# Weight columns of the v projection in a windowed-attention block: 128 token columns per pair of windows in place of 114

## What is computed

```
xn  = layernorm(x)                                  # over the 192 channels
xw  = windows of 7x7 of roll(xn, -3, -3)            # 1024 windows of 49 tokens
q, k, v = xw @ qkv_w + qkv_b                        # 6 heads of 32
o   = softmax(q k^T * scale) v                      # within a window
x   = x + roll back(o @ proj_w + proj_b)
x   = x + gelu(layernorm(x) @ mlp_w1 + mlp_b1) @ mlp_w2 + mlp_b2
```

## Time and profile before

| | |
|---|---|
| median of 3 runs | 2993.93 us (2991.17 to 2994.59) |
| profiled execution | 2994.5 us, span from first to last instruction 2992.4 us |
| TensorE matmuls busy | 2942.3 us, 98% |
| TensorE weight loads busy | 2873.1 us, 96% |
| VectorE busy | 2669.3 us, 89% |
| ScalarE busy | 2276.4 us, 76% |
| GpSimd busy | 1434.7 us, 48% |
| mean granted clock of TensorE | 0.992 |

### The profile page before, as it was taken

The page is one execution under the profiler, slowest core; times in us unless marked ns, Lnnn a source line. Parts: engine busy times, 40 slices in busy tenths (PEclk is TensorE's granted clock), DMA queues, the critical chain, the costliest instruction groups (busy, mean ns, idle before and its releaser), DMA issues.

```text
span 2992.4 us, 115822 instructions
## 1 busy us (share of the span) xinstructions
PE 2942.3 (98%) x43446; PEld 2873.1 (96%) x43446; DVE 2669.3 (89%) x6802; ACT 2276.4 (76%) x4493; POOL 1434.7 (48%) x1678
## 2 busy tenths in 40 slices
PE   6999999999999999999999999999999999999997
PEld 5999999999999999999999999999999999999997
DVE  5899999999999999999999999999999999999994
ACT  3777777777777777777777777777777777877775
POOL 2445454554544455454444545445444554544452
PEclk8999999999999999999999999999999999999998
DMA  1010011001001000100100010010011001001000
GB/s 48 21 31 26 24 28 29 24 25 31 25 24 30 27 24 26 30 24 24 30 26 24 27 29 24 24 31 25 24 28 28 24 26 30 25 24 30 27 21 17
DMA packets 109325, 79.78 MB, mean 27 GB/s; under 512 B 7294, under 2 KB 108782, under 8 KB 109294
## 3 DMA queue, kind: packets, MB, share of 16 engines
q1 hardware_dynamic: 107682, 77.18, 9.6%
q10 hardware_dynamic: 1612, 2.16, 0.2%
HBM read 40.78 MB, written 38.54 MB: 27 GB/s over the span
## 4 chain that ended last, share of the span: by engine, by line
PE 98%; ACT 1%; DVE 1%; ACTq 1%; issue 0%; DVEq 0%
PE ps L855 35%; PE ps L858 16%; PE ps L962 5%; PE ps L886 5%; PE ps L927 5%; PE ps L928 5%; PE ps L935 5%; PE ps L982 5%; PE ps L936 5%; PE ps L929 5%; PE ps L818 3%; PE ps L826 2%; PE ps L943 2%; PE ps L947 1%; PE ps L828 1%
## 5 line engine op out<-in xcount | busy, mean ns | idle before, releaser
L394 POOL TENSOR_TENSOR gl<-g,gh 128x392 fp32r<-128x392 f32 x512 | 566.9, 1129 | 308.5 <-ACT gh L704 308.5
L855 PE MATMUL ps<-zh,w 128*128 128x392 f32 x3072 | 698.7, 342 | 0.6 <-ACT zh L666 0.6
L855 PEld LDWEIGHTS ps<-zh,w 128*128 128x128 f32 x3072 | 551.4, 188 | 0.8 <-ACT zh L666 0.8
L279 POOL TENSOR_TENSOR prob<-prob,rcp 128x588 f32<-128x588 f32 x128 | 152.0, 1187 | 750.2 <-DVE rcp L593 750.2
L698 ACT ACTIVATE g<-ps,biasf 128x392 f32<-128x392 f32 x768 | 396.9, 592 | 131.0 <-PE ps L855 131.0
L855 PE MATMUL ps<-zh1c,wqkv 128*128 128x392 f32 x1536 | 362.6, 345 | 4.0 <-DVE zh1c L452 4.0
L704 ACT ACTIVATE gh<-g 128x392 fp32r<-128x392 f32 x768 | 355.5, 551 | 0.0
L386 POOL CAST zh<-zh1c 128x392 fp32r<-128x392 f32 x256 | 133.7, 522 | 444.9 <-DVE z L442 428.9
L584 DVE TENSOR_TENSOR gl<-g,gh 128x392 fp32r<-128x392 f32 x256 | 289.2, 1168 | 18.3 <-ACT gh L704 18.3
L858 PE MATMUL ps<-wqkv,zh 128*114 128x192 f32 x2048 | 288.4, 268 | 2.5 <-DVE prob L550 2.0
L855 PEld LDWEIGHTS ps<-zh1c,wqkv 128*128 128x128 f32 x1536 | 281.4, 190 | 5.7 <-issue 4.3
(11 more groups left out here) (111 smaller groups left out, 7556.9 us busy)
## 6 DMA issues: line engine op xcount, KB each, us to landing
xin<-in_x SPq DMA_DIRECT2D x128, 147.0 KB
out<-yo SPq DMA_DIRECT2D x128, 147.0 KB
xin<-in_x SPq DMA_DIRECT2D x128, 71.2 KB
out<-yo SPq DMA_DIRECT2D x128, 71.2 KB
xin<-in_x SPq DMA_DIRECT2D x128, 54.8 KB
out<-yo SPq DMA_DIRECT2D x128, 54.8 KB
xin<-in_x SPq DMA_DIRECT2D x128, 18.8 KB
out<-yo SPq DMA_DIRECT2D x128, 18.8 KB
```

The lines of the kernel that those rows point to most:

```text
L394: pool.tensor_tensor(gl[:, m, :], g[:, m, :], gh[:, m, :].bitcast(F32), ALU.subtract)\
L855: last = pe.matmul(dst, cols(w, part), act_, start=(n == 0), stop=(n == 4))
```

## The change

v's stationary operand takes the whole two fields of 64 token columns, 128, where it took 114 (113 and one more); the output is all 128 partitions of the bank, where it was 114. Nothing else is different; what reads v (`values`, line 692) still reads 114 rows.

```
             for p in range(PAIRS):
                 if p % 2 == 0:
                     wait(pe, s_sub, 3, i, p // 2 + 1)
-                last = project(ps[0:PAIR + 1, V + p // 2, 256 * (p % 2):256 * (p % 2) + C], zh1, zl1, wqkv,
+                last = project(ps[:, V + p // 2, 256 * (p % 2):256 * (p % 2) + C], zh1, zl1, wqkv,
                                lambda w, part: w[:, part, 2 * C:3 * C],
-                               tokens=slice(2 * WIDE * p, 2 * WIDE * p + PAIR + 1))
+                               tokens=slice(2 * WIDE * p, 2 * WIDE * (p + 1)))
             last.then_inc(v_done, 1)
```

## The result

The changed kernel takes 3014.33 us (median of 5 runs, 3014.0 to 3016.66) against 2993.93 before, 20.4 us slower; the ratio on record is 1.0072, 95% interval 1.0061 to 1.0084 (the two medians alone give 1.0068). One further run of the kernel before took 3725.34 us in a slow state and stands in neither figure. The forecast was 3011.0 with a range of 3005 to 3024. The profiled execution has a span of 3012.1 us, 19.7 more than before.

A forecast was written before the change was run, and what follows sets the result against it. Added TensorE time (98% busy) is paid except its 0.10 us wait for VectorE's longer path to `x2_done`: 0.23 - 0.10 = 0.13 per iteration, 16.1 us over 124, plus 1.0 for four others, 17.1; forecast 3011.0 us, range 3005 to 3024.

The forecast's parts named there:

- The load paces v, at 0.8 ns a column: v's 20 matmuls per iteration: weight load sets their spacing; 14 more columns cost 11.5 ns each, 0.23 us per iteration.
- No faster load at 128 columns: v's weight loads: 128 columns of this 32-bit type take 188 ns, on the line of shorter loads, despite the skill's rule.
- VectorE's path is 0.10 us longer, and v eats that: Second six transposes (line 962): TensorE waits 0.07 or 0.13 us for `x2_done`; v's 0.23 absorbs it, leaving 0.13.
- Late next is nothing else: After the `x2_done` wait: v's lengthening makes nothing further late, so 0.13 us per iteration is the whole cost.
- start from TensorE's own signals and move with it: GELU, second MLP matmul, q and k: these later stages shift with TensorE, with no added wait.
- The cover behind line 692: ScalarE: line 692 starts 0.23 us later, but the following exponential waited 0.35 for VectorE, so 0.12 of cover is left.
- The 1.0 for the four iterations outside: Four iterations outside 120 to 2930 us, partly at half clock: charged in full, 4 by 0.25 us.
- An iteration: 22.64.: Steady stretch before the change: 22.64 us from one block of 30 wide matmuls to the next.
- the 22.77 given as a sign: Steady stretch after the change: an iteration would be 0.13 us longer, 22.77.
- Full price: Rival at `x2_done`: line 557 moves with TensorE, so no wait is eaten; 29.4 us more, 3023.3; chance 0.10.
- The surplus of 22 ns: Rival at v's matmuls: 128 columns bring the wide matmuls' surplus, 22 ns each; 44 us more, 3038; chance 0.03.
- the faster load: Rival "not slower" at v's loads: faster mode at 128, or 114 already paced as 128; time 2994; chance 0.10.

The follow-up runs named there:

- the last two kernels: Kernel before and changed kernel, each with the `x2_done` wait split and the GELU's fourth low part on VectorE: 2981.46 and 3013.44 us.
- before_rf: Kernel before with VectorE's line 557 (residual, `x2_done`) put ahead of the four jobs of line 442 that prepare the next group: 3101.27 us.

## Why the prediction was right, and what it missed

- *The load paces v, at 0.8 ns a column.* Right: 105 ns at 120 columns, 111 to 112 at 128, and the same iteration with a third of the stream left out. I took 11.5 ns a matmul, 0.23 per iteration; it was 11.7, 0.234.
- *No faster load at 128 columns.* Right: 192 ns a load against 181. The Trainium skill's condition for Fast Weight Load (TensorE: Matmul & The Clock Gate, section on weight-path performance modes) is met here only if this 32-bit type does not count as FP32. The trace shows no faster load at 128; that the type is the reason no run here shows.
- *VectorE's path is 0.10 us longer, and v eats that.* Right: -100 ns in the transposes; no gain in the time when v shrinks (98 columns), full price (32 us) when the wait is taken away beforehand, and line 557 is 8.14 us behind line 602 in both.
- *"Late next is nothing else", "start from TensorE's own signals and move with it".* This step failed, by 20 ns at q and k, although the forecast as a whole was right. GpSimd's fourth line 394 does move with TensorE, but VectorE's line 584 doesn't and is held by it, so line 452 comes 0.25 later and not in its old place. That contention was in the profile before (line 584 took 1180 ns on average where 552 is its own time), and the prediction has no term for it. It is 124 by 0.020 = 2.5 us. Another 6 ns are in lines 927 to 929, which took 3.225 or 3.250 before and always 3.250 after; their cause is open.
- *The cover behind line 692.* Right, with little to spare: line 710 began 0.28 to 0.35 us after line 692 had ended, and now begins 0.04 to 0.12 after it. Nothing was held up by it, as VectorE's 8.146 us from line 602 to line 557 are the same.
- *The sum.* 0.13 per iteration was 0.163, which is 4.1 us more in 124 iterations. The 1.0 for the four iterations outside did not show: the spans grew by 19.7 in all, the 124 alone account for 20.2. The two misses partly cancel, so that 17.1 stands against 20.4 by the medians.
- *"An iteration: 22.64."* That was a single one; the mean was 22.724. The sum doesn't use it, but the 22.77 given as a sign should have read 22.85; it was 22.887.
- *The rivals.* Full price (3023.3) describes the kernel without the wait, not this one. The surplus of 22 ns and the faster load did not come.

## What to carry to other kernels

An engine that is 98% busy by its records can still be off the longest path: look at the spacing of its instructions, and for waits that a record hides. What lengthens it beside the longer path is then cheaper than it looks by the wait, and what shortens it there brings nothing until that wait is gone; what lies on the loop that both paths share counts in full. An iteration that repeats to the nanosecond, as in the last two kernels, is a sign that no such wait is left. When an edit moves one engine against another, follow every pair of jobs of VectorE and GpSimd that lie side by side, since their overlap moves too. And if columns of a stationary operand are only padding, each of them costs as much as a used one wherever the load paces the group.

## What the runs showed of the hardware

VectorE and GpSimd hold each other up in some pairs and not in others. Line 584 (two inputs in SBUF) took 552 ns without line 394 beside it and up to 1403 with it; GpSimd's fourth line 394 took 1.43 us beside line 584, where the first three took 1.03. Line 442 took 371 and, in the order of `before_rf`, where it lies partly beside line 394, 735 on average. Line 429, which ran beside jobs of line 394 in every kernel, took 340 to 348 on average throughout.

The Trainium skill (SBUF — State Buffer, section SBUF: two separate sides) says that the two engines share one pair of ports as an exclusive lock, taken by a VectorE operation with two SBUF inputs or in a 2-port mode, and that the one that starts first keeps it for its whole instruction. As to which pairs contend the traces agree, if line 442 runs in a 2-port mode, which no run here shows. As to who keeps the lock they don't bear it out by the records: the first line 584 began 0.48 us before the fourth line 394 in the kernel before and 0.73 before it in the changed one, and yet lasted 1.02 and 1.27 us.
